# One-core transformer block: the feed-forward part and the agents' rows run batch by batch inside the linear-attention stage

## What is computed

```
h = token_mixer(x)                      # attention-free mixer, 256 rows of 256 per batch
h = concat([h, txt], axis=1)            # 288 rows
h = h + linear_attention(LN(h))         # 8 heads of 64, decayed sums over time, gated, W_O
h = h + (quantise(LN(h) @ H, 4 bits) @ ternary(W).T)          # the feed-forward part
h = h + agents(LN(h))                   # see below
h = h + mixture(LN(h))                  # 8 experts of 192, top 2, plus shared experts

agents: a = LN(h) @ (Wq.T @ w_conv) per row; s = sum over rows of a * LN(h);
        two softmaxes over [8, 256] and [8, 288]; one row per batch is added to all its rows
```

## Time and profile before

| | us |
|---|---|
| runs: 741.69, 749.14, 749.04; median | 749.04 |
| profiled execution | 747.01 |
| its span, first to last instruction | 744.9 |
| attention stage, about | 121 to 403 |
| feed-forward stage | 404 to 475 |
| agents' stage | 475 to 519 |
| TensorE / VectorE / ScalarE / GpSimd busy | 598.7 / 449.8 / 235.2 / 210.4 |

### The profile page before, as it was taken

How to read it: one execution, slowest core, us unless ns; L and a number is a source line. 1 busy time by engine, 2 the same in 40 slices (tenths; PEclk the granted TensorE clock), 3 DMA queues, 4 the chain that set the end, 5 groups by cost and what they waited for, 6 DMA issues and landing times. The chain is left out here.

```text
span 744.9 us, 10658 instructions
## 1 busy us (share of the span) xinstructions
PE 598.7 (80%) x3627; PEld 471.4 (63%) x3627; DVE 449.8 (60%) x1037; ACT 235.2 (32%) x490; POOL 210.4 (28%) x269
## 2 busy tenths in 40 slices
PE   2899861889889898988985676477698799999983
PEld 2666530857677676857764565144477689989773
DVE  1378874767777776767684698455766543222246
ACT  5112210315233241514321565600341035554410
POOL 4236554121000000101001121550301247777710
PEclk9999975889999999999998689857599799999998
DMA  6311151000000000000002400000210013333366
GB/s 172 95 34 52 42 148 42 1 1 1 1 1 1 1 1 1 1 2 0 2 1 72 183 0 1 0 1 0 86 43 0 29 50 105 101 104 103 100 217 185
DMA packets 27606, 36.96 MB, mean 50 GB/s; under 512 B 4774, under 2 KB 22950, under 8 KB 27558
## 3 DMA queue, kind: packets, MB, share of 16 engines
q1 hardware_dynamic: 23334, 24.78, 11.0%
q0 software_dynamic: 4224, 11.54, 5.0%
HBM read 25.95 MB, written 10.35 MB: 49 GB/s over the span
## 5 line engine op out<-in xcount | busy, mean ns | idle before, releaser
L506 PE MATMUL ps<-b_x_hi,wa_hi 128*128 128x288 f32 x192 | 58.1, 303 | 6.5 <-DVE b_qk L969 6.5
L2260 DVE TENSOR_TENSOR f_hg<-ps,f_si 128x192 f32<-128x192 f32 x43 | 15.4, 358 | 69.3 <-ACT f_si L2067 69.3
L507 PE MATMUL ps<-b_x_lo,wa_hi 128*128 128x288 f32 x192 | 57.1, 297 | 0.0
L508 PE MATMUL ps<-b_x_hi,wa_lo 128*128 128x288 f32 x192 | 57.0, 297 | 0.0
L2320 POOL DMA_INDIRECT f_xg<-x_rows,r_src_i x43 | 41.7, 970 | 38.6 <-DVE r_src_i L2186 14.7
L885 ACT CAST b_y_hi<-b_yt 128x256 fp32r<-128x256 f32 x32 | 13.0, 407 | 115.2 <-DVE b_yt L941 115.2
L750 PE MATMUL ps<-b_qk 64*128 64x160 f32 (+2 forms) x384 | 41.6, 334 | 7.6 <-DVE b_x_lo L986 5.9
L954 DVE TENSOR_TENSOR b_a<-ps,decay 128x1024 f32<-128x1024 f32 x32 | 38.4, 1219 | 13.2 <-PE ps L750 13.2
L1953 PE MATMUL ps<-w,f_ht 96*128 x172 | 44.6, 381 | 1.3 <-ACT f_ht L2079 1.2
L1090 POOL TENSOR_TENSOR b_z<-b_z,b_qk 128x288 f32<-128x288 f32 x16 | 14.8, 941 | 102.2 <-DVE b_qk L969 102.2
L1083 POOL TENSOR_TENSOR b_rstd<-b_ve,mhalf 128x2 f32<-128x2 f32 (+1 forms) x8 | 5.9, 737 | 130.1 <-DVE b_ve L491 130.1
(11 more groups left out here) (374 smaller groups left out, 1611.7 us busy)
## 6 DMA issues: line engine op xcount, KB each, us to landing
d_x_hi<-y_rows SPq DMA_DIRECT2D x18, 256.0 KB, 4.1
w1raw<-in_W_t SPq DMA_DIRECT2D x8, 384.0 KB, 6.4
x_rows<-d_xn SPq DMA_DIRECT2D x6, 384.0 KB, 2.5
a_xt<-in_x_t SPq DMA_DIRECT2D x8, 256.0 KB, 3.5
a_xfl<-in_x_flat SPq DMA_DIRECT2D x8, 256.0 KB, 2.8
out<-hres SPq DMA_DIRECT2D x16, 128.0 KB, 3.8
w<-in_W_t SPq DMA_DIRECT2D x8, 192.0 KB, 5.2
w1raw<-in_Ws_t SPq DMA_DIRECT2D x1, 768.0 KB, 8.4
```

Source lines behind the costliest of these rows:

```text
L506: nc.tensor.matmul(out, x_hi, w_hi, start=start, stop=False)
L507: nc.tensor.matmul(out, x_hi, w_lo, start=False, stop=False)
L508: return nc.tensor.matmul(out, x_lo, w_hi, start=False, stop=stop)
```

## The change

`feed_forward` is gone as a stage. `linear_attention` becomes `attention_and_ffn`, whose step b also does the feed-forward part and the agents' rows of unit u = b-1: the two tiles of that batch, and the text tile after batches 3 and 7. Two more steps follow the last batch. The six pairs now write banks `(4, 0, 4, 0, 6, 4)`, values 6 and 7, and banks 2 and 3 belong to the units. `x_hi`/`x_lo` are doubled, `turn_x` comes before the projections, and the scale of the first LayerNorm moves to ScalarE. The spread of the reciprocals is written as three parts and two added ones, and `divide` is three operations. W1, the router's weights and W2 are loaded in the agents' stage, K and V of the agents in the attention stage. Several buffers share space; in `mixture` only the place of buffers changes.

```diff
-            return (4, 6, 2, 4, 6, 2)[i]
+            return (4, 0, 4, 0, 6, 4)[i]
...
+        steps = range(-2, B + 2)
...
+            for b in steps:
+                u = b - 1
+                if is_batch(b):
+                    scores(b, 1)
+                    values(b, 0)
+                if is_batch(u):
+                    turn_unit(u)
+                if is_batch(b):
+                    scores(b, 2)
+                    values(b, 1)
+                    scores(b, 3)
+                if is_batch(u):
+                    rotate(u)
+                if is_batch(b):
+                    values(b, 2)
+                    values(b, 3)
+                if b == B:
+                    for n in range(B - 1):
+                        agent_sums(n)
+                if is_batch(b + 2):
+                    turn_x(b + 2)
+                if is_batch(b + 1):
+                    projections(b + 1)
+                elif is_batch(u):
+                    turn_q(u)
+                    ternary(u)
+                if is_batch(b):
...
+                    output(b, 0)
+                if b == -1:
+                    ffn_weights()
+                if is_batch(b + 1):
+                    denominators(b + 1)
+                    scores(b + 1, 0)
+                    spread_out(b + 1)
+                if is_batch(b):
+                    output(b, 1)
...
+            def projections(b):
+                pe.wait_ge(lo_done, b + 1)
+                ge(pe, masked, NP * b)
+                pair(b, 0)
+                ge(pe, y_done, NP * b)
...
+                value_rows(b, (0, 1))
+                if b >= 2:
+                    turn_q(b - 2)
+                pe.wait_ge(lo_done, min(b + 2, B))
+                pair(b, 1)
+                pe.wait_ge(phi_done, NP * b + 1)
...
+                pair(b, 2)
+                if b >= 2:
+                    ternary(b - 2)
+                pe.wait_ge(phi_done, NP * b + 2)
+                pair(b, 3)
+                pe.wait_ge(v_read, v_count(b) + 1)
+                pair(b, 4)
+                pe.wait_ge(phi_done, NP * b + 3)
+                pair(b, 5)
...
             def round_w1(b):
                 nc.scalar.copy(part_of(g["w1_hi"], b), part_of(g["w1raw"], b)).then_inc(w_rounded, 1)
-            round_w1(0)
-            round_w1(1)
             act.wait_ge(dve_done, 1)
             nc.scalar.activation(ex[:], ps[0:B, 4, 0:D], ACT.Exp, bias=mx[:, 0:1],
                                  accum_out=su[:, 0:1]).then_inc(act_done, 1)
-            for b in range(2, NGR):
+            act.wait_ge(w1_in, 16 * (E + 1))
+            for b in range(NGR // 2):
                 round_w1(b)
             act.wait_ge(dve_done, 5)
             nc.scalar.activation(pr[:], ps[0:B, 7, 0:T], ACT.Exp, bias=mx[:, 1:2],
                                  accum_out=su[:, 1:2]).then_inc(act_done, 1)
+            for b in range(NGR // 2, NGR):
+                round_w1(b)
```

More of the change, by code:

```diff
@@ L837, in step @@
                     spread_out(b + 1)
[L838 removed]
+                if is_batch(b):
                     output(b, 1)
[L840 to L843 removed]
+                    if ends(b):
+                        output_text(b)
+            agent_sums(B - 1)
         @block.scalar
@@ L849, in _, with norm @@
             act.wait_ge(bias_in, 16 * NP)
-            def evacuate(b):
-                nc.scalar.activation(warm[:], g["gam"][:, 0:1], ACT.Exp)
+            def norm(b):
+                act.wait_ge(rstd_done, 2 * b + 2)
+                ge(act, x_turned, b)
+                for t in range(NT if starts(b) else 2):
+                    last = nc.scalar.activation(xn[:, t, :] if t < 2 else xn_text[:],
+                                                hres[:, 2 * b + t if t < 2 else text_tile(b), :], ACT.Identity,
+                                                bias=shift[:, t, :], scale=rstd[:, t, :])
+                last.then_inc(xn_done, 1)
@@ new lines, in round_unit, with scaled_rows @@
+            def round_unit(u):
+                act.wait_ge(f_turned, u + 1)
+                n = len(unit(u))
+                nc.scalar.copy(of_unit(f_hi, n), turned_rows(n)).then_inc(f_hi_done, 1)
+            def scaled_rows(u):
+                act.wait_ge(inv_done, u + 1)
+                n = len(unit(u))
+                for t in range(n):
+                    last = nc.scalar.activation(qm[:, t, :], tile_rows(n)[:, t, :], ACT.Identity,
+                                                bias=roundc[:], scale=xinv[:, t:t + 1])
+                last.then_inc(scaled, 1)
@@ new lines, in _ @@
+            for b in steps:
+                u, n = b - 1, b + 1
+                if is_batch(b):
+                    mask(b, 1)
+                    take(b, 0)
+                if is_batch(b + 2):
+                    norm_sums(b + 2)
+                if is_batch(u):
+                    split_unit(u)
+                if is_batch(b):
+                    mask(b, 2)
+                    take(b, 1)
+                    mask(b, 3)
+                if is_batch(u):
+                    scale(u)
+                if is_batch(b):
+                    take(b, 2)
+                    take(b, 3)
+                if is_batch(u - 1):
+                    agents(u - 1)
+                if is_batch(b + 2):
+                    split_x(b + 2)
+                if is_batch(u):
+                    quantise(u)
```

954 lines of the change are left out of this document (453 added, 501 removed).

## The result

The changed kernel took 776.76 us (median of 4 runs, 773.94 to 777.73) against 747.41 us for the kernel before: ratio 1.040, 95% interval 1.0335 to 1.0466. It is slower by 4%, outside the predicted range of 737 to 765. The profiled execution has a span of 775.2 us against 744.9, so 30.3 us are to be found. They are read from windows of both traces, cut at the same instructions: the end of the first gate, of the second, of the eighth, the first VectorE operation of the agents' stage, the first of the mixture.

What follows compares the result with a forecast made beforehand. TensorE was taken to set the attention step. Start +4.7, first step -1.4, six steps +26.2, tail -35.0 and agents' stage -2.1 gave 739.4 us; clock falls of +12 made 751.4, median forecast 752, range 737 to 765.

Steps and rivals of the forecast that it cites:

- Start and first step: Attention stage's opening: first gate at 161.8 instead of 157.1 us (+4.7), then a first step of 33.5 against 34.9 (-1.4).
- The walk through a step: Attention step with a unit, instruction by instruction at steady clock: 35.8 us instead of 31.4; six steps +26.2.
- the clock's term: Attention stage: a TensorE clock fall in each of six unit steps, 2.0 us each, +12.
- upper bound of 3.1: Most a clock fall could cost per unit step, from the stretch at 158.2 to 165.0 us; lower bound nothing.
- rival C: Half clock through the first part of all seven unit steps: 7 x 3.6 = 25 us, total 765; chance 0.26.
- the sum: Whole kernel: steady-clock terms total -7.6 us, giving 739.4; with +12 for the clock, 751.4 against 747.0 profiled.
- The count of quiet steps: Attention stage of the kernel before: four steps of seven kept 2.4 GHz in spite of waits of 0.9 us.
- the 2.9: Attention stage: loss in us per step from which rival C decides, at a total of 757.
- The tail: From the eighth gate to the agents' stage: 55.3 us instead of 90.3, so -35.0.
- The agents' stage: Two W1 casts ahead of the first exponential go, -2.1 us; W1 lands 14.4 after the first issue, at no cost.
- the 2.5 that I had named and not taken: Agents' stage: us that W2's two MB would add if they mixed with W1's loads; left out of the total.
- The nothing that I took for W2: Agents' stage: W2, issued behind W1 on one queue, was to cost nothing, as a ring's descriptors are taken in order.

Runs made afterwards that it cites:

- e2: Changed kernel with eight unread 128x512 products filling TensorE's wait ahead of the unit's turn in seven steps; ratio 1.015 to the kernel before.
- e8: Changed kernel with four unread 128x512 products in the wait ahead of the unit's turn in seven steps; ratio 1.0085 to the kernel before.
- e10: Kernel before, with TensorE made to wait behind values 0 of each batch for two unused GpSimd memsets; ratio 1.038 to the kernel before.
- e1: Changed kernel with the unit's turn moved behind the second pair of scores and values, its split and rotation later; ratio 0.987 to the kernel before.
- e5: Changed kernel with later unit's turn, earlier agents' sums, and six W1 casts behind the second exponential; ratio 0.984 to the kernel before.
- e9: As e5, with the third exponential, its reciprocal and their product also ahead of the W1 casts; ratio 0.980 to the kernel before.

## Why the prediction was wrong

- **Start and first step.** 161.7 was predicted as 161.8; the first step is 34.5 instead of 33.5.
- **The walk through a step** held within 1.2 us. e2 has the order of the changed kernel at a clock of 1.00: three of its steps, two odd batches among them, take 115.2 us, the prediction's 3 x 35.75 and 4.5 give 111.8. The unit's statistics (2.3 us behind the gate), the place of the wait (5.8), its length (2.15 for 2.3), the phi's wait (1.0 for 1.1) and the turn of x (13.45 for 13.05) are right; the rest is lost at the step's end, where the spread in two parts is over 1.4 us behind the inversion instead of 1.0.
- **The step that failed is the clock's term**: "I take 2.0, the mean of the three seen: +12". That a fall would follow the unit's turn in each step was right, and e2, e8 and e10 show that the wait causes it. Its price was not: 3.5 a step in the mean, 20.8 in the six steps, and 5.1 in one, above the upper bound of 3.1 that I had put on it. That bound came from a fall of 6.8 us in the kernel before; at five of the seven turns the half clock lasted about 10 us. The term also left out the seventh turn, unit 6's in the tail, where e2 takes back 4.9 us more: 25.6 against 12. So rival C, half clock through the whole first part in all seven, was the case that came, and its 3.6 a step fits.
- **How much of the miss that is.** The profiled span grew by 30.3 us where the sum gave 4.4. Of these 25.9, the clock's term is 13.6, the walk of the six steps 8.1 (in it the falls that e2 still has), the rest of the tail 1.7, the first step 1.0, the part from the agents' stage on 1.5. With the clock at its price the sum is 765.0, rival C's figure and the edge of the range; the walk and the tail took the time beyond it.
- **The count of quiet steps** was one too high: three steps of the kernel before had a clock of 1.00, the fourth had a fall at its end (0.97). And rival C, which counts seven falls, decides from 2.4 us each (17.1 over 7); the 2.9 is for six.
- **The Trainium skill**, TensorE: Matmul & The Clock Gate, section A second HAM failure mode: psum-queue depth-cycling, had the clock swing where TensorE idles briefly between groups. The trace agrees: 0.85 to 0.91 in all steps of the changed kernel, 1.00 in three of e2. But not every brief wait did it: e8 has one of 0.58 to 1.59 us at each turn and no fall behind it.
- **The tail** took 61.9 instead of 55.3. Unit 6's turn has the same wait and fall in it: in e2, where this wait is filled, the tail takes 57.1. The sums took 8.18 us at half clock, 6.6 were taken.
- **The agents' stage** gave 1.7 of 2.1 us. W1 landed 2.2 later than forecast, near the 2.5 that I had named and not taken. The nothing that I took for W2, by the order of the ring, is not borne out: up to the landing the queues moved 291 GB/s for 16.6 us, 4.8 MB, and W1 is 3.9, so part of W2 went ahead of W1's last piece; no run leaves W2 out. The casts then held the exponential up by 1.8. The first exponential gave 1.2 instead of 2.1, and 1.9 came from VectorE's product of 16 columns, which the prediction did not have. That this came was luck of the order: in e1, e2 and e8, where W1 landed a little earlier in the stage, the same product is held up again.
- **What was not in the prediction at all** is what TensorE's idle time was worth moving: the wait of 2.15 us was seen, priced and left standing, and the lines moved in e1 take back more than the whole loss (0.987 against 1.040).

Open: why the half clock lasts 3.4 to 6.8 us in e10 and mostly 10 in the changed kernel behind a wait of about the same length, and what starts the falls that are left in e5 (in four of six steps, each begun ahead of a gate; none in the last two, with the same order).

## What to carry to other kernels

When a change puts work of another chain into TensorE's program, look for the first instruction whose input is not ready, and put it where it is; a wait of 2 us there cost itself and 2.3 to 3.5 us more for the clock in each pass, or 4.2 in all in the kernel before. Price such a fall by how much TensorE work follows it at half speed, not by the falls that the old kernel happened to have. Filling a wait with products nobody reads is a quick test of whether the wait or the clock is the loss. The version with the turn, the sums and the casts in better places (e9) is 2% faster than the kernel before, where the change as given is 4% slower.

## What the runs showed of the hardware

A wait of TensorE of about 2 us (1.97 in e10, mostly 2.15 in the changed kernel) inside a stage that ran mostly at a clock of 1.00 went with a clock of 0.50 right behind it in every step, in two kernels, and filling it took the fall away (e2). Waits of 0.8 to 1.0 in the same steps often had no fall, and those of 0.58 to 1.59 us at the turn in e8 had none.

A VectorE product with both sources in SBUF waits while GpSimd's subtraction from SBUF runs: 2.77 and 5.84 us in e1 and 4.23 in e5 for operations of 0.17 or 0.18, the last one ending with the last subtraction. One with a source in PSUM took 0.29 us in the midst of the subtractions. The Trainium skill, SBUF — State Buffer, section SBUF: two separate sides, says this: the two engines share a pair of ports, which one instruction holds to its end, and a VectorE operation with two SBUF inputs needs it when GpSimd's reads SBUF. The rows agree. The kernel before has it too: the operation that takes 0.17 us in the changed kernel took 2.08 there, and the 1.9 us are part of what the agents' stage gained.
